# The last Fourier layer's second complex mixing by three real products, and scan records loaded three chunks ahead

## The chip, the cores and the metric

The kernel runs on one core of one Trainium2 chip. The metric is the device time of one execution in microseconds. A core has TensorE (PE, its weight loads are PEld), VectorE (DVE), ScalarE (ACT), GpSimd (POOL) and SyncE (SP), which issues most of the transfers.

## What is computed

Four layers over `x` of 4 x 512 x 64 x 64, each behind a group normalisation and with a residual path folded in: a recurrent layer with test-time training (a scan over 256 chunks of 16 tokens), a Fourier layer, a channel gate, and a second Fourier layer. The change touches the first and the last:

```python
# scan, one chunk of 16 tokens for each of 8 heads and 4 images
Z1 = xk @ W1c + b1c
grad = _ln_l2_bwd(Z1, xv - xk, g, bb)
W1n = W1c - (last_eta * xk).swapaxes(-1, -2) @ grad
b1n = b1c - (last_eta * grad).sum(-2, keepdims=True)
...
# Fourier layer
spec = jnp.fft.rfft2(x, axes=(2, 3), norm='ortho')
xr, xi = (out.real, out.imag)
or_ = einsum('bkihw,kio->bkohw', ar, w[0]) - einsum('bkihw,kio->bkohw', ai, w[1]) + b[0]
oi_ = einsum('bkihw,kio->bkohw', ai, w[0]) + einsum('bkihw,kio->bkohw', ar, w[1]) + b[1]
o1r, o1i = relu(cmul(xr, xi, w1, b1))
o2r, o2i = cmul(o1r, o1i, w2, b2)
out_c = (o2r + 1j * o2i) * origin
return jnp.fft.irfft2(out_c, s=(H, W), axes=(2, 3), norm='ortho')
```

## The kernel before

Everything is fp32. `fourier_back` is the last Fourier layer. It works on 16 units (4 images x 4 groups of 128 channels), one after the other; channels lie on the partitions. A unit's half spectrum is `spec[k]`, 33 slots of 64 frequencies, real and imaginary. It is mixed in NCH = 9 chunks: six of 256 columns, then three of 192. Each chunk goes through these steps:

- `mix1`: three real products on TensorE (`once1` = w_re times (x_re + x_im) in `psA[0]`, and two more in `psA[1]`), with the sum x_re + x_im made by GpSimd (`sums`);
- `copy_once1` on ScalarE takes `once1` out of PSUM, `combine_hidden` on VectorE adds it to both halves of `psA[1]`, and `relu` on ScalarE (two activations) makes `hidden[q]`;
- `mix2`: four real products on TensorE, two into `psB[0]` and two into `psB[1]`;
- `terms` on VectorE: four scalar_tensor_tensor, each adding the bias to a half of `psB` and multiplying by a half of `spec`, into `prod[q]`;
- `gate` on GpSimd: one difference and one sum of `prod[q]`, back into `spec[k]`.

While unit u is mixed, the rows of unit u - 1 (still in `half`) are transformed back, one batch of 512 columns a chunk: transposes (`turn_rows`), `evacuate` on ScalarE, products (`transform_rows`), `row_back` on VectorE. Behind the nine chunks the columns of unit u follow (`turn_columns`, `transform_columns`). The first unit has no rows to turn. Every engine runs a fixed list of instructions in program order, and semaphores (`Signal`, here counted by step) join them. TensorE's list in a chunk is mix2(c), transform_rows(c), turn_rows(c+2), mix1(c+2); mix2(c) waits for hidden(c) and for terms(c-1).

`scan_and_read` is the recurrent layer. Chunk s of the scan works on `record[s % 4]`, a 392 KB load from HBM (`load_record`, a ring of RING = 4). The recurrence is kept for two groups g of two images. TensorE transposes the keys of the next chunk (`turn_keys`, L2299), multiplies keys by the state (`project_k`) and adds to the state (`update`, L2328); the signal `state_ps[g]` counts the updates. SyncE goes chunk by chunk (`body`): the load of a later record (L1840), the tiles' loads and stores, and the two stores of the gradients, each of which waits for its `stored_sb[g]`. Records are `turn_keys`'d late in an odd chunk, and early in an even one.

Of the kernel before, what the change touches and what calls it, by code (L numbers as in the profile page):

```python
# [649 lines left out]
def fourier_back(nc, name, s_in, x_out, weights, biases, d, coef):  # L650

    o_view = x_out.rearrange("b (k c) h w -> (b k) c (h w)", c=P)
# [6 lines left out]
    with ExitStack() as ctx:  # L659
# [12 lines left out]
        wdif = sb("weights_dif", [P, CT, P])  # L672
# [6 lines left out]
        hidden = [sb(f"hidden{k}", [P, 2, CW]) for k in range(2)]  # L679
        once1 = sb("once1", [P, CW])  # L680
        prod = [sb(f"prod{k}", [P, 2, 2, CW]) for k in range(2)]
# [28 lines left out]
        mix2_ps = sig("mix2_ps", 2 * NCH)  # L710
# [67 lines left out]
        def _(pool):  # L778
            def combine_weights(ct):
                pool.wait_ge(w_loaded[ct].sem, w_loaded[ct].at(0, 32))  # L780
                nc.gpsimd.tensor_tensor(wneg[:, ct], zeros[:], wt[:, ct, 0:4:3], ALU.subtract).then_inc(neg_begun.sem, 1)  # L781
                nc.gpsimd.tensor_tensor(wdif[:, ct], wt[:, ct, 1], wt[:, ct, 0], ALU.subtract)
                pool.wait_ge(neg_begun.sem, neg_begun.at(0, ct + 1))
                nc.gpsimd.tensor_tensor(wneg[:, ct, 0], wneg[:, ct, 0], wt[:, ct, 1], ALU.subtract).then_inc(combined.sem, 1)

            def sums(u, k):
                pool.wait_ge(mix1_ps.sem, mix1_ps.at(u, 0))
                for n, (s0, s1) in enumerate(PARTS):
                    pool.wait_ge(scaled.sem, scaled.at(u, n + 1))
                    if n == 0:  # L790
                        pool.wait_ge(dc_added.sem, dc_added.at(u, 1))
                    nc.gpsimd.tensor_tensor(xsum[:, s0:s1], spec[k][:, s0:s1, 0, :], spec[k][:, s0:s1, 1, :],  # L792
                                            ALU.add).then_inc(xsum_sb.sem, 1)

# [12 lines left out]
            def unit(u, it, k, ct, first):  # L807
                cf = coef[:, bass.ds(u, 1), :].rearrange("p o e -> p (o e)")
                nc.gpsimd.tensor_tensor(bias_re[k][:], bias[:, ct, 2:3], cf[:, 2:3], ALU.add).then_inc(bias_made.sem, 1)
                sums(u, k)  # L810
                if first:
                    for n in range(1, CT):
                        combine_weights(n)
                for c in range(NCH):
                    gate(u, k, (k * NCH + c) % 2, c, cf)
# [6 lines left out]
        def _(act):  # L822
# [21 lines left out]

            def relu(u, k, ct, c):
                n = width(c)
                q = (k * NCH + c) % 2
                act.wait_ge(pre_sb.sem, pre_sb.at(u, c + 1))
                for r in range(2):
                    done = nc.scalar.activation(hidden[q][:, r, 0:n], hidden[q][:, r, 0:n], ACT.Relu, bias=bias[:, ct, r:r + 1])  # L850
                done.then_inc(hidden_sb.sem, 1)
# [4 lines left out]
            def unit(u, it, k, ct, first, final=False):  # L856
# [5 lines left out]
                for c in range(NCH):  # L862
                    if not first and c + 2 < NB1:
                        row_back(u, k, c + 2)
                    if c + 2 < NCH:
                        copy_once1(u, c + 2)
                        relu(u, k, ct, c + 2)
# [16 lines left out]
        def _(dve):  # L884
# [17 lines left out]
            def terms(u, k, q, c, adds):  # L902
                s0, s1 = CHUNKS[c]
                n = width(c)
                dve.wait_ge(prod_sb.sem, prod_sb.at(u, c - 1))
                for r, add in enumerate(adds):
                    dve.wait_ge(mix2_ps.sem, mix2_ps.at(u, 2 * c + r + 1))
                    src = psB[r][:, 0:n].rearrange("p (s h) -> p s h", h=H)
                    for e in range(2):
                        done = v.scalar_tensor_tensor(prod[q][:, r, e, 0:n].rearrange("p (s h) -> p s h", h=H), src, add,  # L910
                                                      spec[k][:, s0:s1, e, :], ALU.add, ALU.mult)
                done.then_inc(terms_sb.sem, 1)

            def unit(u, it, k, ct, first):
# [3 lines left out]
                for c in range(NCH):  # L918
                    q = (k * NCH + c) % 2
                    terms(u, k, q, c, (bias_re[k][:], bias[:, ct, 3:4]))  # L920
                    if c < NB1 and not first:
                        row_back(u, it, k, c)
                    if c + 2 < NCH:
# [15 lines left out]
        def _(pe):  # L939
# [34 lines left out]
            def mix1(u, k, ct, c):  # L974
# [7 lines left out]
                pe.matmul(psA[1][:, CW:CW + n], wdif[:, ct], x[:, :, 0, :], start=True, stop=True).then_inc(mix1_ps.sem, 1)  # L982

            def mix2(u, k, ct, c):
# [3 lines left out]
                if c:  # L988
                    pe.wait_ge(terms_sb.sem, terms_sb.at(u, c))
                for r, (wa, wb) in enumerate(((wt[:, ct, 2], wneg[:, ct, 1]), (wt[:, ct, 3], wt[:, ct, 2]))):  # L990
                    pe.matmul(psB[r][:, 0:n], wa, hidden[q][:, 0, 0:n], start=True, stop=False)  # L991
                    pe.matmul(psB[r][:, 0:n], wb, hidden[q][:, 1, 0:n], start=False, stop=True).then_inc(mix2_ps.sem, 1)  # L992
# [630 lines left out]
def scan_and_read(nc, T, d, x_in, rec, q_in, grad, x_out, chan_stats):  # L1623
# [15 lines left out]
    with ExitStack() as ctx:  # L1639
# [198 lines left out]
        def _(sp):  # L1838
# [26 lines left out]
            for s in range(2):  # L1865
# [4 lines left out]
            def body(at, scan):  # L1870
                s, c, v, p = at.s, at.c, at.v, at.p
                if scan:

                    for g in range(GR):
                        sp.wait_ge(state_ps[g].sem, state_ps[g].at(s, -1))
                    load_record((c + 2) % RING, s + 2)
# [25 lines left out]
            for r in range(RING):  # L1902
                sp.wait_ge(rec_in[r].sem, rec_in[r].at(SC * 2 + (r < 2), 0))
# [827 lines left out]
```

## Time and profile before

| | before |
|---|---|
| runs, us | 5644.74, 5626.67, 5643.87 (median 5643.87) |
| the profiled execution | 5642.43 us, its span 5640.3 us |
| PE / DVE / ACT / POOL busy | 93% / 74% / 46% / 48% of the span |
| mean granted TensorE clock | 0.971 |
| scan, 1579 to 3850 us | 2271 us |
| last Fourier layer's units, 4838.5 us to the end | 801.8 us |

The busy share says how much of the span an engine had an instruction in work. TensorE's records overlap and their ends are modelled, so for it the distance from start to start is the better measure of what an instruction costs; for the other engines it is the distance too where two follow each other without a wait.

### The profile page before, as it was taken

How to read it: one execution, taken by the hardware profiler on the slowest of the kernel's cores; microseconds unless marked ns; L12 is line 12 of the kernel's file. 1: busy time of each engine (PE TensorE's matmuls, PEld its weight loads, DVE VectorE, ACT ScalarE, POOL GpSimd, SP SyncE). 2: the span in 40 equal slices, each digit the busy share in tenths (PEclk: the TensorE clock that was granted, in tenths of full speed). 3: DMA queues.
4: the chain of work that ended last, by engine and by line, in shares of the span. 5: the costliest groups of instructions: out<-in, count | busy, mean ns of one | idle time of the engine just before them, and what ended most of it. 6: DMA issues, size and time to landing. Idle time of an engine off the chain costs nothing. (4 is left out here: it accounts for less than half of the span.)

```text
span 5640.3 us, 144710 instructions
## 1 busy us (share of the span) xinstructions
PE 5236.2 (93%) x44534; PEld 4008.5 (71%) x44534; DVE 4165.7 (74%) x14714; ACT 2613.6 (46%) x7573; POOL 2684.5 (48%) x4382
## 2 busy tenths in 40 slices
PE   5999999999969999999999999997999997799999
PEld 2444444444448888888888888886888896699888
DVE  4766667656558888888888888886788888566665
ACT  0111111111146666666666666664555554454444
POOL 1444444444435655565556565662444444333332
PEclk8999999999959999999999999998999999899999
DMA  4434444333324444444444444443312121222121
GB/s 182 163 123 156 149 148 163 125 118 125 117 80 119 123 123 123 121 123 122 121 122 122 120 122 118 123 124 88 131 77 92 78 92 47 88 92 80 76 90 76
DMA packets 599465, 645.80 MB, mean 114 GB/s; under 512 B 172976, under 2 KB 503096, under 8 KB 587736
## 3 DMA queue, kind: packets, MB, share of 16 engines
q1 hardware_dynamic: 440712, 491.44, 27.4%
q10 hardware_dynamic: 157904, 144.22, 7.6%
q8 instruction: 390, 6.39, 0.5%
q14 instruction: 459, 3.76, 0.2%
HBM read 357.56 MB, written 278.00 MB: 113 GB/s over the span
## 5 line engine op out<-in xcount | busy, mean ns | idle before, releaser
L1613 PE MATMUL proj_ps<-proj_w_sb,proj_h 128*128 128x512 f32 x3072 | 1347.2, 596 | 0.0
L1613 PEld LDWEIGHTS proj_ps<-proj_w_sb,proj_h 128*128 128x128 f32 x3072 | 577.4, 190 | 743.4 <-issue 724.7
L1516 DVE SCALAR_TENSOR_TENSOR proj_lin<-proj_ps,proj_rstd,proj_wbias_sb 128x512 f32<-128x512 f32 x384 | 283.0, 746 | 496.9 <-PE proj_ps L1613 490.9
L1928 POOL TENSOR_TENSOR scan_b_step<-scan_core,scan_rate_last 128x128 f32<-128x128 f32 x512 | 325.3, 635 | 631.4 <-DVE scan_core L2188 631.4
L2397 PE MATMUL scan_ps_y<-scan_o_t,proj_wo_sb 128*128 128x128 f32 x4096 | 569.7, 282 | 2.1 <-ACT scan_o_t L2031 2.1
L2397 PEld LDWEIGHTS scan_ps_y<-scan_o_t,proj_wo_sb 128*128 128x128 f32 x4096 | 500.0, 192 | 32.6 <-ACT scan_o_t L2031 2.6
L1997 ACT ACTIVATE scan_square<-scan_ps_z 128x64 f32<-128x64 f32 x1024 | 219.9, 220 | 490.5 <-PE scan_ps_z L2316 464.3
L1431 POOL TENSOR_TENSOR proj_gk<-proj_rec,proj_gain_sb 128x256 f32<-128x256 f32 x256 | 181.4, 730 | 529.5 <-DVE proj_rec L1537 529.5
L1425 POOL TENSOR_TENSOR proj_by_cos<-proj_lin,proj_rope 128x512 f32<-128x512 f32 x256 | 335.4, 1324 | 164.8 <-DVE proj_lin L1516 123.1
L2328 PE MATMUL scan_ps_w<-scan_step,scan_record 64*128 64x128 f32 x4088 | 359.1, 296 | 9.0 <-DVE scan_step L2193 8.7
L1936 POOL TENSOR_TENSOR scan_b_sum<-scan_b_step,scan_b_sum 128x128 f32<-128x128 f32 x512 | 318.4, 622 | 46.5 <-POOL scan_b_step L1928 8.6
L1990 ACT COPY scan_state_w<-scan_ps_w 128x512 f32<-128x512 f32 x480 | 279.1, 582 | 121.0 <-PE scan_ps_w L2328 118.7
L2328 PEld LDWEIGHTS scan_ps_w<-scan_step,scan_record 64*128 64x128 f32 x4088 | 278.7, 193 | 40.4 <-DVE scan_step L2193 14.2
L418 DVE SCALAR_TENSOR_TENSOR fourier_boxes<-fourier_spec,fourier_tab 128x256 f32<-128x256 f32 (+3 forms) x544 | 302.5, 593 | 0.5
L550 PE MATMUL fourier_psD<-fourier_mats,fourier_turned 128*128 128x128 f32 x2148 | 291.9, 278 | 11.0 <-DVE fourier_spec L452 8.4
L288 POOL TENSOR_TENSOR fourier_spec<-fourier_prod 128x256 f32<-128x256 f32 (+1 forms) x144 | 129.6, 900 | 356.5 <-DVE fourier_prod L439 356.5
L800 POOL TENSOR_TENSOR fourier_spec<-fourier_prod 128x256 f32<-128x256 f32 (+1 forms) x144 | 98.4, 683 | 411.6 <-DVE fourier_prod L910 411.6
L550 PEld LDWEIGHTS fourier_psD<-fourier_mats,fourier_turned 128*128 128x128 f32 x2148 | 273.4, 193 | 23.0 <-ACT fourier_turned L319 14.8
L2167 DVE TENSOR_TENSOR scan_zg<-scan_ps_z,scan_gain 128x128 f32<-128x128 f32 x512 | 146.0, 285 | 187.1 <-ACT scan_square L1997 162.4
L951 PE MATMUL fourier_psD<-fourier_mats,fourier_turned 128*128 128x128 f32 x2080 | 277.6, 277 | 4.1 <-ACT fourier_turned L826 4.1
L951 PEld LDWEIGHTS fourier_psD<-fourier_mats,fourier_turned 128*128 128x128 f32 x2080 | 262.0, 191 | 14.2 <-ACT fourier_turned L826 8.1
L826 ACT COPY fourier_turned<-fourier_psT 128x512 f32<-128x512 f32 (+1 forms) x272 | 153.6, 566 | 244.1 <-PE fourier_psT L943 244.1
(326 smaller groups left out, 13269.3 us busy)
## 6 DMA issues: line engine op xcount, KB each, us to landing
scan_record<-records SPq DMA_DIRECT2D x258, 392.0 KB
records<-proj_rec ACTq DMA_DIRECT2D x256, 392.0 KB, 3.7
spectra<-fourier_spec SPq DMA_DIRECT2D x16, 2112.0 KB, 6.5
fourier_spec<-spectra SPq DMA_DIRECT2D x16, 2112.0 KB, 8.7
proj_h<-x SPq DMA_DIRECT2D x32, 1024.0 KB, 6.5
queries<-proj_q ACTq DMA_DIRECT2D x128, 256.0 KB, 3.7
gradients<-scan_stored SPq DMA_DIRECT2D x512, 64.0 KB
scan_q_in<-queries SPq DMA_DIRECT2D x128, 256.0 KB, 7.7
```

The costliest lines, as they stand in the source:

```text
L418: v.scalar_tensor_tensor(boxes[:, g % 2, 0:nj * 2 * nf].rearrange("p (j e f) -> p j e f", j=nj, e=2), spec[q][:, s, :, f], 1.0, tab[:, j, ...
L550: done = pe.matmul(psD[t % 2][:, col:col + P], turned[t % 2][:, j * P:(j + 1) * P], mat, start=True, stop=True)
L951: done = pe.matmul(psD[q][:, col:col + P], turned[q][:, j * P:(j + 1) * P], mat, start=n == 0, stop=n == len(terms) - 1)
L1425: g_.tensor_tensor(by_cos[q][:, n].rearrange("p (a e) -> p a e", e=32), lin[q][:, n].rearrange("p (a e) -> p a e", e=32), cos, ALU.mult).t ...
L1516: v.scalar_tensor_tensor(lin[q][:, n], ps[q][n][:], rstd[k][:, j:j + 1], T.wbias[:, n], ALU.mult, ALU.add).then_inc(lin_sb.sem, 1)
L1613: last = pe.matmul(ps[j % 2][n][:], h[k][:, ct, j * P:(j + 1) * P], T.w[:, n, ct], start=ct == 0, stop=ct == CT - 1)
L1928: v.tensor_tensor(b_step[g][:], core[g][:], rate_last[g][:, :, 2:3].broadcast_to([P, PB, HD]), ALU.mult).then_inc(b_step_sb[g].sem, 1)
L1936: v.tensor_tensor(b_sum[g][(c + 1) % RING][:], b_step[g][:], b_sum[g][c % RING][:], ALU.add).then_inc(b_sum_sb[g].sem, 1)
L1990: a.copy(state_of(g, at)[:].rearrange("p r b a e -> p r (b a e)"), ps_w[:, :, g].rearrange("p r b a e -> p r (b a e)")).then_inc(state_sb[ ...
L1997: a.activation(square[:, g, b], ps_z[g][:, b * HD:(b + 1) * HD], ACT.Square, accum_out=ssq[g][:, b:b + 1]).then_inc(ssq_sb[g].sem, 1)
L2328: done = pe.matmul(ps_w[:, r, g, b].rearrange("p a e -> p (a e)"), record[at.ring][rows, PB * g + b, 0:2 * HD], step[g][rows, b].rearrange ...
L2397: pe.matmul(ps_y[:, n], T.wo[:, ct, n * P:(n + 1) * P], o_t[:, ct], start=ct == 0, stop=False)
```

## The change

In `fourier_back` the second mixing is done like the first: GpSimd makes `hsum` = h_re + h_im (`sum_hidden`), TensorE makes three products (`psB[1]` holds two, `psB[0]` the one with `hsum`), ScalarE takes the latter out of PSUM (`copy_once2`), and VectorE adds bias, `psB[1]` and `once2` into `mixed` in SBUF (`combine_mixed`) and multiplies it by the spectrum with two tensor_tensor of 512 columns (`terms`), both of whose inputs are in SBUF. `mix2(c)` waits for `mixed(c-1)` in place of terms(c-1), and its last product for `hsum`. In the scan, three records are loaded ahead in place of two, and the load waits for all updates up to the chunk before in place of the one before that.

```diff
+            def sum_hidden(u, q, c):
+                n = width(c)
+                pool.wait_ge(hidden_sb.sem, hidden_sb.at(u, c + 1))
+                if c >= 2:
+                    pool.wait_ge(mix2_ps.sem, mix2_ps.at(u, c - 1))
+                nc.gpsimd.tensor_tensor(hsum[q][:, 0:n], hidden[q][:, 0, 0:n], hidden[q][:, 1, 0:n], ALU.add).then_inc(hsum_sb.sem, 1)
...
                 for c in range(NCH):
-                    gate(u, k, (k * NCH + c) % 2, c, cf)
+                    sum_hidden(u, (k * NCH + c) % 2, c)
+                    if c:
+                        gate(u, k, (k * NCH + c - 1) % 2, c - 1, cf)
+                gate(u, k, (k * NCH + NCH - 1) % 2, NCH - 1, cf)
...
+            def copy_once2(u, c):
+                n = width(c)
+                act.wait_ge(mix2_ps.sem, mix2_ps.at(u, c + 1))
+                nc.scalar.copy(once2[:, 0:n], psB[0][:, 0:n]).then_inc(once2_sb.sem, 1)
...
                 for c in range(NCH):
+                    copy_once2(u, c)
                     if not first and c + 2 < NB1:
                         row_back(u, k, c + 2)
                     if c + 2 < NCH:
...
-            def terms(u, k, q, c, adds):
+            def combine_mixed(u, q, c, adds):
+                n = width(c)
+                dve.wait_ge(once2_sb.sem, once2_sb.at(u, c + 1))
+                for r, add in enumerate(adds):
+                    done = v.scalar_tensor_tensor(mixed[q][:, r, 0:n], psB[1][:, r * CW:r * CW + n], add, once2[:, 0:n],
+                                                  ALU.add, ALU.add)
+                done.then_inc(mixed_sb.sem, 1)
+
+            def terms(u, k, q, c):
                 s0, s1 = CHUNKS[c]
                 n = width(c)
+                dve.wait_ge(mixed_sb.sem, mixed_sb.at(u, c + 1))
                 dve.wait_ge(prod_sb.sem, prod_sb.at(u, c - 1))
-                for r, add in enumerate(adds):
-                    dve.wait_ge(mix2_ps.sem, mix2_ps.at(u, 2 * c + r + 1))
-                    src = psB[r][:, 0:n].rearrange("p (s h) -> p s h", h=H)
-                    for e in range(2):
-                        done = v.scalar_tensor_tensor(prod[q][:, r, e, 0:n].rearrange("p (s h) -> p s h", h=H), src, add,
-                                                      spec[k][:, s0:s1, e, :], ALU.add, ALU.mult)
+                for r in range(2):
+                    pv = prod[q][:, r, :, 0:n].rearrange("p e (s h) -> p e s h", h=H)
+                    mv = mixed[q][:, r, 0:n].rearrange("p (s h) -> p s h", h=H).unsqueeze(1).broadcast_to([P, 2, s1 - s0, H])
+                    done = v.tensor_tensor(pv, mv, spec[k][:, s0:s1].rearrange("p s e h -> p e s h"), ALU.mult)
                 done.then_inc(terms_sb.sem, 1)
...
                     q = (k * NCH + c) % 2
-                    terms(u, k, q, c, (bias_re[k][:], bias[:, ct, 3:4]))
+                    combine_mixed(u, q, c, (bias_re[k][:], bias[:, ct, 3:4]))
                     if c < NB1 and not first:
                         row_back(u, it, k, c)
+                    terms(u, k, q, c)
                     if c + 2 < NCH:
                         combine_hidden(u, q, c + 2)
...
                 if c:
-                    pe.wait_ge(terms_sb.sem, terms_sb.at(u, c))
-                for r, (wa, wb) in enumerate(((wt[:, ct, 2], wneg[:, ct, 1]), (wt[:, ct, 3], wt[:, ct, 2]))):
-                    pe.matmul(psB[r][:, 0:n], wa, hidden[q][:, 0, 0:n], start=True, stop=False)
-                    pe.matmul(psB[r][:, 0:n], wb, hidden[q][:, 1, 0:n], start=False, stop=True).then_inc(mix2_ps.sem, 1)
+                    pe.wait_ge(mixed_sb.sem, mixed_sb.at(u, c))
+                pe.matmul(psB[1][:, 0:n], wneg[:, ct, 1], hidden[q][:, 1, 0:n], start=True, stop=True)
+                pe.matmul(psB[1][:, CW:CW + n], wdif[:, ct, 1], hidden[q][:, 0, 0:n], start=True, stop=True)
+                pe.wait_ge(hsum_sb.sem, hsum_sb.at(u, c + 1))
+                pe.matmul(psB[0][:, 0:n], wt[:, ct, 2], hsum[q][:, 0:n], start=True, stop=True).then_inc(mix2_ps.sem, 1)
...
-            for s in range(2):
+            for s in range(3):
                 load_record(s, s)
...
                     for g in range(GR):
-                        sp.wait_ge(state_ps[g].sem, state_ps[g].at(s, -1))
-                    load_record((c + 2) % RING, s + 2)
+                        sp.wait_ge(state_ps[g].sem, state_ps[g].at(s, 0))
+                    load_record((c + 3) % RING, s + 3)
```

Left out: the buffers and signals that these lines name, the weights' sums for the second mixing (`wneg`, `wdif`, made by GpSimd), and the last waits of SyncE.

On ScalarE, inside a unit's chunks, a chunk's work before is one transposed batch out (`fourier_turned`), one `once1` (from `psA`) and the two activations of relu:

```order
L850 ACTIVATE fourier_hidden<-fourier_hidden,fourier_bias 128x256 x2
L826 COPY fourier_turned<-fourier_psT 128x512
L843 COPY fourier_once<-fourier_psA 128x256
L850 ACTIVATE fourier_hidden<-fourier_hidden,fourier_bias 128x256 x2
L826 COPY fourier_turned<-fourier_psT 128x512
```

The same place in the changed kernel; `fourier_once<-fourier_psB` is `once2`:

```order
L873 ACTIVATE fourier_hidden<-fourier_hidden,fourier_bias 128x256 x2
L866 COPY fourier_once<-fourier_psB 128x256
L844 COPY fourier_turned<-fourier_psT 128x512
L861 COPY fourier_once<-fourier_psA 128x256
L873 ACTIVATE fourier_hidden<-fourier_hidden,fourier_bias 128x256 x2
L866 COPY fourier_once<-fourier_psB 128x256
```

The copy of `once2` for chunk c + 1 stands right behind the relu of chunk c + 2.

On VectorE, the same chunk before (`fourier_prod` is terms, `fourier_x` is row_back, `fourier_hidden` is combine_hidden of chunk c + 2):

```order
L910 SCALAR_TENSOR_TENSOR fourier_prod<-fourier_psB,fourier_bias_re,fourier_spec 128x256 x2
L907 REGISTER_ALU
L910 SCALAR_TENSOR_TENSOR fourier_prod<-fourier_psB,fourier_bias,fourier_spec 128x256 x2
L891 REGISTER_ALU
L892 COPY fourier_x<-fourier_psD 128x512
L896 REGISTER_ALU
L899 TENSOR_TENSOR fourier_hidden<-fourier_psA,fourier_once 128x512
```

And after (`fourier_mixed` is combine_mixed):

```order
L930 SCALAR_TENSOR_TENSOR fourier_mixed<-fourier_psB,fourier_bias_re,fourier_once 128x256
L930 SCALAR_TENSOR_TENSOR fourier_mixed<-fourier_psB,fourier_bias,fourier_once 128x256
L915 REGISTER_ALU
L916 COPY fourier_x<-fourier_psD 128x512
L942 TENSOR_TENSOR fourier_prod<-fourier_mixed,fourier_spec 128x512 x2
L920 REGISTER_ALU
L923 TENSOR_TENSOR fourier_hidden<-fourier_psA,fourier_once 128x512
```

Two of the four scalar_tensor_tensor are gone, two tensor_tensor of twice the width stand behind row_back, and combine_hidden of chunk c + 2 is still the last of a chunk.

## Rows read from the trace of the kernel before

**Rows 1.** The page: busy time of each engine, share of the span, instructions.
```profile
PE 5236.2 (93%) x44534; PEld 4008.5 (71%) x44534; DVE 4165.7 (74%) x14714; ACT 2613.6 (46%) x7573; POOL 2684.5 (48%) x4382
```

**Rows 2.** Windows, busy us of PE PEld DVE ACT POOL, clock: scan, last Fourier.
```profile
1579.00:3850.00 2271.00, 2147.31 (x29634) 1863.80 (x29633) 1910.14 (x9628) 1519.47 (x5322) 1335.87 (x2803) 0.97 0.42 119
4838.50:5640.30 801.80, 766.23 (x5129) 714.53 (x5127) 502.70 (x991) 379.58 (x791) 280.00 (x402) 0.99 0.21 81
```

**Rows 3.** Waits of PE in the scan: total us, times, longest us.
```profile
PE scan_ps_turn L2299 <- DMA scan_record<-records: 64.8, 72, 3.6
...
PE scan_ps_z L2316 <- ACT scan_k_t L2005: 9.1, 33, 0.7
PE scan_ps_w L2328 <- DVE scan_step L2193: 8.7, 15, 1.7
```

**Rows 4.** Timeline of PE in the scan, four chunks: start us, length us.
```profile
2335.59 0.65 PE L2299 MATMUL scan_ps_turn<-proj_ident_sb,scan_record 128*128 128x128 f32 x4
...
2337.87 0.71 PE L2328 MATMUL scan_ps_w<-scan_step,scan_record 64*128 64x128 f32 x8
...
2348.21 0.72 PE L2328 MATMUL scan_ps_w<-scan_step,scan_record 64*128 64x128 f32 x8
...
2352.34 0.66 PE L2299 MATMUL scan_ps_turn<-proj_ident_sb,scan_record 128*128 128x128 f32 x4
...
2357.52 0.66 PE L2299 MATMUL scan_ps_turn<-proj_ident_sb,scan_record 128*128 128x128 f32 x4 [0.87 <-DMA scan_record<-records]
...
2370.18 0.66 PE L2299 MATMUL scan_ps_turn<-proj_ident_sb,scan_record 128*128 128x128 f32 x4
```

**Rows 5.** Timeline of SyncE's queue in the same chunks.
```profile
2339.85 0.62 SPq L1840 DMA_DIRECT2D scan_record<-records  x1
...
2349.70 0.62 SPq L1840 DMA_DIRECT2D scan_record<-records  x1
```

**Rows 6.** Timeline of PE in one unit's mixing, last Fourier layer.
```profile
5171.15 0.60 PE L991 MATMUL fourier_psB<-fourier_hidden,fourier_weights 128*128 128x256 f32 x2
...
5184.21 0.59 PE L991 MATMUL fourier_psB<-fourier_hidden,fourier_weights 128*128 128x256 f32 x2
5184.64 0.59 PE L992 MATMUL fourier_psB<-fourier_hidden,fourier_weights_neg 128*128 128x256 f32 x2
...
5188.56 0.59 PE L991 MATMUL fourier_psB<-fourier_hidden,fourier_weights 128*128 128x256 f32 x2
...
5203.56 1.04 PE L943 MATMUL fourier_psT<-fourier_ident,fourier_spec 128*128 128x128 f32 x8
```

**Rows 7.** Timelines of DVE and ACT there; the last two rows: another unit.
```profile
5184.48 0.69 DVE L899 TENSOR_TENSOR fourier_hidden<-fourier_psA,fourier_once 128x512 f32<-128x512 f32 x1 [1.11 <-PE fourier_psA L982]
5185.20 0.91 ACT L850 ACTIVATE fourier_hidden<-fourier_hidden,fourier_bias 128x256 f32<-128x256 f32 x2 [1.23 <-DVE fourier_hidden L899]
5185.27 0.88 DVE L910 SCALAR_TENSOR_TENSOR fourier_prod<-fourier_psB,fourier_bias_re,fourier_spec 128x256 f32<-128x256 f32 x2
...
5187.03 0.69 DVE L892 COPY fourier_x<-fourier_psD 128x512 f32<-128x512 f32 x1
...
4879.36 0.91 ACT L850 ACTIVATE fourier_hidden<-fourier_hidden,fourier_bias 128x256 f32<-128x256 f32 x2
4880.17 0.36 ACT L843 COPY fourier_once<-fourier_psA 128x256 f32<-128x256 f32 x1
```

**Rows 8.** Groups by form: busy us, mean ns, idle before.
```profile
L418 DVE SCALAR_TENSOR_TENSOR fourier_boxes<-fourier_spec,fourier_tab 128x256 f32<-128x256 f32 x306 | 238.5, 814 | 0.0
...
L1506 DVE TENSOR_TENSOR proj_rec<-proj_gk,proj_lin 128x512 f32<-128x512 f32 x128 | 103.1, 806 | 10.3 <-POOL proj_rec L1432 9.0
...
L2246 DVE TENSOR_TENSOR scan_zn<-scan_zgain,scan_hrstd 128x512 f32<-128x512 f32 x128 | 88.6, 692 | 4.4
...
L899 DVE TENSOR_TENSOR fourier_hidden<-fourier_psA,fourier_once 128x384 f32<-128x384 f32 x48 | 26.8, 558 | 29.7 <-PE fourier_psA L982 29.7
...
L801 POOL TENSOR_TENSOR fourier_spec<-fourier_prod 128x256 f32<-128x256 f32 x96 | 69.8, 727 | 0.0
```

More of the change, by code:

```diff
@@ L671, in fourier_back @@
         wneg = sb("weights_neg", [P, CT, 2, P])
-        wdif = sb("weights_dif", [P, CT, P])
+        wdif = sb("weights_dif", [P, CT, 2, P])
         bias = sb("bias", [P, CT, 4])
@@ L679, in fourier_back @@
         hidden = [sb(f"hidden{k}", [P, 2, CW]) for k in range(2)]
+        hsum = [sb(f"hsum{k}", [P, CW]) for k in range(2)]
         once1 = sb("once1", [P, CW])
+        once2 = sb("once2", [P, CW])
+        mixed = [sb(f"mixed{k}", [P, 2, CW]) for k in range(2)]
         prod = [sb(f"prod{k}", [P, 2, 2, CW]) for k in range(2)]
@@ L709, in fourier_back @@
         hidden_sb = sig("hidden_sb", NCH)
-        mix2_ps = sig("mix2_ps", 2 * NCH)
+        hsum_sb = sig("hsum_sb", NCH)
+        mix2_ps = sig("mix2_ps", NCH)
+        once2_sb = sig("once2_sb", NCH)
+        mixed_sb = sig("mixed_sb", NCH)
         terms_sb = sig("terms_sb", NCH)
@@ L780, in combine_weights @@
                 pool.wait_ge(w_loaded[ct].sem, w_loaded[ct].at(0, 32))
-                nc.gpsimd.tensor_tensor(wneg[:, ct], zeros[:], wt[:, ct, 0:4:3], ALU.subtract).then_inc(neg_begun.sem, 1)
-                nc.gpsimd.tensor_tensor(wdif[:, ct], wt[:, ct, 1], wt[:, ct, 0], ALU.subtract)
+                re, im = wt[:, ct, 0:4:2], wt[:, ct, 1:4:2]
+                nc.gpsimd.tensor_tensor(wneg[:, ct], zeros[:], re, ALU.subtract).then_inc(neg_begun.sem, 1)
+                nc.gpsimd.tensor_tensor(wdif[:, ct], im, re, ALU.subtract)
                 pool.wait_ge(neg_begun.sem, neg_begun.at(0, ct + 1))
-                nc.gpsimd.tensor_tensor(wneg[:, ct, 0], wneg[:, ct, 0], wt[:, ct, 1], ALU.subtract).then_inc(combined.sem, 1)
+                nc.gpsimd.tensor_tensor(wneg[:, ct], wneg[:, ct], im, ALU.subtract).then_inc(combined.sem, 1)
             def sums(u, k):
@@ L981, in mix1 @@
                 pe.matmul(psA[1][:, 0:n], wneg[:, ct, 0], x[:, :, 1, :], start=True, stop=True)
-                pe.matmul(psA[1][:, CW:CW + n], wdif[:, ct], x[:, :, 0, :], start=True, stop=True).then_inc(mix1_ps.sem, 1)
+                pe.matmul(psA[1][:, CW:CW + n], wdif[:, ct, 0], x[:, :, 0, :], start=True, stop=True).then_inc(mix1_ps.sem, 1)
             def mix2(u, k, ct, c):
@@ L1902, in _ @@
             for r in range(RING):
-                sp.wait_ge(rec_in[r].sem, rec_in[r].at(SC * 2 + (r < 2), 0))
+                sp.wait_ge(rec_in[r].sem, rec_in[r].at(SC * 2 + (r < 3), 0))
             for g in range(GR):
```

## The prediction

> **What bounds the kernel now.** I read the page first: TensorE is busy for 93% of the span, the others for half to three quarters [rows 1]. The change touches two stages, so I took a window of each [rows 2]. In both TensorE is the engine without gaps: 2147 of 2271 us in the scan, 766 of 802 us in the last Fourier layer, at a granted clock of 0.97 and 0.99. There the reader is to see that only what TensorE does, or waits for, sets the time.
>
> What it waits for in the scan is in the list of waits [rows 3]: 64.8 us, in 72 waits, for the record that the transposes of L2299 read. All else that is named there is under 10 us each. The timeline shows one such wait and one chunk pair without it [rows 4]: from 2335.59 to 2352.34, two chunks take 16.75 us; from 2352.34 to 2370.18, with a wait that is named with 0.87 us, 17.84 us. The record came late because its load was issued at 2349.70 [rows 5] and the transposes began at 2357.52, that is 7.8 us later, as soon as it had landed.
>
> In the last Fourier layer a chunk takes 4.35 us of TensorE (5184.21 to 5188.56), and of these a product of 256 columns takes 0.43 us (5184.21 to 5184.64) [rows 6]. In the same chunk VectorE works 0.69 + 2 x 0.88 + 0.69 = 3.1 us and waits for TensorE for the rest; ScalarE's relus take 0.91 us [rows 7]. From the first product of mix2(0) to the first transpose behind mix2(8) it is 32.41 us (5171.15 to 5203.56) [rows 6].
>
> **The scan.** The load of record s + 3 now waits for the updates of chunk s - 1, and stands where that of s + 2 stood. Either way it refills the ring's buffer that the update of four chunks before set free; what moves is its place in SyncE's queue, one chunk earlier. Is SyncE held up there, with the stores and loads behind it? The update of the second group ended at 2337.87 + 0.71 = 2338.58 and at 2348.21 + 0.72 = 2348.93 [rows 4], and SyncE came to its loads at 2339.85 and 2349.70 [rows 5]: the new wait is over before SyncE arrives, so it costs nothing, and would cost what little those two are apart if the stores were faster. The load that TensorE waited for at 2357.52 would be issued at 2339.85 in place of 2349.70, 9.9 us earlier; the wait of 0.87 us is covered ten times over. So the row's 64.8 us go at the most, or up to 80 if each of the 72 costs 0.2 us more than it is named with, as the pair above does (17.84 - 16.75 = 1.09). At the least nothing is gained, if another wait follows at once. Against that stands the pair without the wait: it ran in 16.75 us with the same work. I take **-62 us**.
>
> **The Fourier layer, TensorE alone.** Of four products one goes: per unit 6 x 0.43 and 3 x 0.33 (in proportion to 192 columns), 3.6 us, 57 us over 16 units. That would be the gain if TensorE stayed the bound.
>
> **The Fourier layer, the new chain.** ScalarE copies `once2` of chunk c + 1 behind the relu of chunk c + 2 (the order shown above). That relu waits for combine_hidden(c + 2), which VectorE does last in chunk c, behind combine_mixed(c), row_back(c) and terms(c). And combine_mixed(c + 1) waits for the copy. So from one combine_mixed to the next everything is in series, with nothing of it overlapped:
>
> - combine_mixed: two scalar_tensor_tensor with one input in PSUM and one in SBUF, as now two of L910: 0.88 us [rows 7];
> - row_back 0.69 us and combine_hidden 0.69 us, as now [rows 7];
> - terms: two tensor_tensor of 128x512 with both inputs in SBUF. The nearest row, the same form with a broadcast input, is 692 ns; the same form under much work of GpSimd is 806 ns [rows 8]. I take 0.69, so 1.38 us; the other end is 1.61;
> - relu: 0.03 us from combine_hidden's end (5184.48 + 0.69 to 5185.20), then 0.91 us [rows 7];
> - the copy of once2: as that of once1, 0.36 us, begun 0.10 us before the relus' record ends (4879.36 + 0.91 against 4880.17) [rows 7];
> - hand-off from ScalarE to VectorE: 0.06 us, my estimate, from 0.03 in the row above and up to 0.1.
>
> The sum is 4.9 us a chunk of 256 columns. TensorE has 4.35 - 0.43 = 3.92 us of work in it and waits for mixed(c) for 1.0 us. GpSimd has three operations of 0.73 us [rows 8], 2.2 us: hsum right behind the relus and over before TensorE's third product needs it, the gate behind terms. Nobody waits for GpSimd.
>
> A unit, from mix2(0) on: three products 1.29, 0.16 until the last is in PSUM, the copy 0.36 and the hand-off 0.06 make 1.9 us to combine_mixed(0). Then four steps of 4.9; the fifth with combine_hidden at 558 ns [rows 8] in place of 692 and relus narrower in proportion, 4.66; the sixth 4.6; the seventh with combine_mixed and terms of 192 columns, 4.2. Behind them combine_mixed(7) 0.74, a hand-off of 0.06 and three products of 0.33 make 1.8. The sum is 1.9 + 19.6 + 4.66 + 4.6 + 4.2 + 1.8 = 36.7 us against 32.4: **+4.3 us a unit**, 65 us over 15 units. The first unit has no row_back: a chunk goes from seven products, 3.0 us, to 4.2 us, about +6 us. The columns behind the mixing are as before, and they cover terms(8) and gate(8), which end later now by some 2 us. Together **+71 us**. The bounds: with terms at 1.61 us, +30 more (0.23 x 9 x 15); with overlaps of records that I have not credited (0.1 at each pair of like instructions, 0.2 a chunk), 27 less.
>
> The few sums of weights on GpSimd lie ahead of the first unit or behind its `sums`: under 2 us, within the rest.
>
> **Sum.** On the profiled execution's 5642.4 us (1.5 under the median of the runs): 5642.4 + 71 - 62 = **5651 us**. Two large terms nearly cancel. What a measurement of this kernel can tell from no change is 0.3%, 17 us: from 5627 to 5661 it is the same.
>
> **The rivals.**
>
> *Terms collide with GpSimd.* The new tensor_tensor read two inputs in SBUF, where L910 read one. A row of this kernel with two inputs in SBUF beside a busy GpSimd, L418, takes 814 ns for 256 columns, where L910 takes 0.44 [rows 7, 8]: 0.37 more. Paid by both operations in 144 chunks it is +107 us: 5758 us. It decides if GpSimd has an operation in work when terms starts. By the chain above it has not: hsum is over 0.4 us after combine_mixed starts, and the gate waits for terms. Chance 0.07. The page "SBUF — State Buffer" of the Trainium skill, section "Who interferes with whom", gives such a rule: a VectorE instruction with two SBUF inputs and a GpSimd instruction that reads SBUF exclude each other. L418 agrees, but no row of before has this meeting in the last layer.
>
> *The scan does not give back what it waits.* Another wait takes the record's place: ScalarE's key copy or VectorE's step, 9 us each now [rows 3], grow as TensorE comes earlier; VectorE is busy for 1910 of 2271 us [rows 2], 84%, and would be at 87%. Then the scan gains 15 us and the result is 5642 + 71 - 15 = 5698 us. Against it: the pair at 16.75 us. Chance 0.17.
>
> *A shorter chain and all of the waits.* Overlaps uncredited above (-27) and -78 in the scan: 5608 us. Chance 0.22.
>
> *The chain does not bind*, TensorE stays the bound and the change is what it says: 5642 - 57 - 62 = 5523 us. It needs ScalarE's copy ahead of the relu, which the order denies. Chance 0.06.
>
> The forecast itself has 0.48, with a range of its own from 5630 to 5672.
>
> **How the numbers follow.** The range reaches over the forecast, the scan's rival and the shorter chain: 5600 to 5705, and leaves out the collision and the chain that doesn't bind. Faster by over 0.3%: most of 0.22 and 0.06, 0.25. Slower: 0.17 + 0.07 and the upper third of the near cases, 0.32. Same: 0.43.
>
> **What the profile after would show.** In the last layer: TensorE's busy share down from 96% to about 83%, its waits there named with fourier_mixed, some 1.0 us each; ScalarE's copy of once2 right behind the relus; the distance between two combine_mixed 4.9 us; terms at 0.69 us; the mixing of a unit 36.7 us. In the scan: no wait of L2299 for the record, 16.75 us a pair, 2209 us in all. I am wrong if the once2 copy is not behind the relu, if terms is over 0.75 us, if TensorE falls to the lower clock in its 1.0 us waits, or if another wait stands where the record's stood.

## The result: 0.9% faster, and the profile after

The changed kernel takes 5586.5 us (median of 4 runs, 5580.0 to 5592.0), the one before 5641.4 us in the same comparison (4 runs, 5626.7 to 5644.7). The ratio is 0.9907, with a 95% interval from 0.9886 to 0.9928: 55 us faster. The forecast was 5651 us with a range from 5600 to 5705, so the time lies under the range.

The page of the changed kernel (its span is 5584.1 us), which answers to [rows 1]:

```profile
PE 5170.9 (93%) x44246; PEld 3939.1 (71%) x44246; DVE 4205.8 (75%) x14714; ACT 2642.5 (47%) x7717; POOL 2782.7 (50%) x4526
```

The windows of the two stages after, which answer to [rows 2] (stretch, its length, busy us of PE, PEld, DVE, ACT and POOL, granted clock, DMA share, GB/s):

```profile
1579.00:3755.00 2176.00, 2109.06 (x29640) 1845.25 (x29638) 1911.77 (x9633) 1520.26 (x5324) 1337.28 (x2806) 0.99 0.44 125
4741.80:5584.10 842.30, 738.21 (x4848) 662.77 (x4848) 533.38 (x992) 410.08 (x939) 382.94 (x551) 0.98 0.20 79
```

The scan's window went from 2271 to 2176 us with VectorE's busy time unchanged (1910 and 1912 us). The last Fourier layer grew from 802 to 842 us, and TensorE now has 738 us of records in it, 28 fewer than before, and many more gaps. Measured more closely, by the starts of the key transposes of the first and the last chunk, the scan went from 2265.5 to 2169.7 us, **-96**; by the first product of the first unit and the end, the last layer went from 806.6 to 842.3 us, **+36**. All that lies outside these two stages, which the change does not touch, is together 4 us longer, with no row that explains it. On the profiled execution's 5642.4 us that makes 5586, and the profiled execution after took 5586.3 us. Both stage figures are of one execution before and one after. That matters for the scan: the five other kernels below that have the new loads took 2171.4 to 2178.0 us for the same scan, and the one with the old loads 2253.0 in place of 2265.5, so by the traces the scan gained between 75 and 96 us.

TensorE's waits in the scan after (line, what it waited for: total us, times, longest), which answer to [rows 3]:

```profile
PE scan_ps_w L2361 <- DVE scan_step L2226: 17.9, 25, 1.7
PE scan_ps_z L2342 <- issue: 17.3, 6, 3.3
```

The wait for the record, 64.8 us in 72 times before, is not in the list any more. The wait for VectorE's step, the rival's candidate, grew from 8.7 to 17.9 us: possibly some of what the record's wait hid. The transposes of the keys in the timeline of PE, which answer to [rows 4], and the records' loads in SyncE's queue, which answer to [rows 5], both some 430 us further on in the scan:

```profile
2763.77 0.60 PE L2332 MATMUL scan_ps_turn<-proj_ident_sb,scan_record 128*128 128x128 f32 x4
...
2780.51 0.60 PE L2332 MATMUL scan_ps_turn<-proj_ident_sb,scan_record 128*128 128x128 f32 x4
```

```profile
2764.07 0.97 SPq L1873 DMA_DIRECT2D scan_record<-records  x1
...
2768.20 4.34 SPq L1918 DMA_DIRECT2D gradients<-scan_stored  x2
```

From 2763.77 to 2780.51 a pair of chunks takes 16.74 us. The record that is used at 2780.51 was issued at 2764.07, 16.4 us ahead. For the same chunk of the kernel before, load and use were 2828.13 and 2835.60, 7.5 us apart, with a named wait:

```profile
2828.13 0.62 SPq L1840 DMA_DIRECT2D scan_record<-records  x1
```

```profile
2835.60 0.66 PE L2299 MATMUL scan_ps_turn<-proj_ident_sb,scan_record 128*128 128x128 f32 x4 [1.01 <-DMA scan_record<-records]
```

Over the scan the median distance from load to use for these chunks (every other one) went from 8.1 to 17.1 us, and for those between from 13.2 to 19.4 us. SyncE's own waits show what the load was moved past:

```profile
SPq L1918 <- POOL scan_stored L1972: 958.0, 417, 4.7
```

In the last layer the list of TensorE's waits (after the first products) is led by the new chain:

```profile
PE fourier_psB L1022 <- DVE fourier_mixed L930: 63.3, 82, 2.1
```

That is 0.8 us for one wait, where 1.0 was forecast. TensorE is busy for 88% of this stage (738 of 842 us), where about 83% was forecast.

And here is a turn of it, in the timelines of DVE and ACT, which answer to [rows 7]:

```profile
5110.08 0.48 DVE L930 SCALAR_TENSOR_TENSOR fourier_mixed<-fourier_psB,fourier_bias_re,fourier_once 128x256 f32<-128x256 f32 x1 [1.23 <-ACT fourier_once L866]
5110.48 0.47 DVE L930 SCALAR_TENSOR_TENSOR fourier_mixed<-fourier_psB,fourier_bias,fourier_once 128x256 f32<-128x256 f32 x1
5110.87 0.68 DVE L916 COPY fourier_x<-fourier_psD 128x512 f32<-128x512 f32 x1
5111.47 1.28 DVE L942 TENSOR_TENSOR fourier_prod<-fourier_mixed,fourier_spec 128x512 f32<-128x512 f32 x2
5112.67 0.68 DVE L923 TENSOR_TENSOR fourier_hidden<-fourier_psA,fourier_once 128x512 f32<-128x512 f32 x1
5113.39 0.91 ACT L873 ACTIVATE fourier_hidden<-fourier_hidden,fourier_bias 128x256 f32<-128x256 f32 x2 [2.58 <-DVE fourier_hidden L923]
5114.20 0.35 ACT L866 COPY fourier_once<-fourier_psB 128x256 f32<-128x256 f32 x1
5114.58 0.48 DVE L930 SCALAR_TENSOR_TENSOR fourier_mixed<-fourier_psB,fourier_bias_re,fourier_once 128x256 f32<-128x256 f32 x1 [1.23 <-ACT fourier_once L866]
```

Every link stands in the order that the prediction gave, and each names the one before it: VectorE idles 1.23 us for ScalarE's copy, and ScalarE idles 2.58 us for combine_hidden. From 5110.08 to 5114.58 a chunk takes 4.50 us, not 4.9. The records' lengths are the ones forecast (terms 1.28 for two, relus 0.91, copy 0.35). But an instruction of VectorE that has nothing to wait for starts about 0.08 us before the record ahead of it ends: 5112.67 lies before 5111.47 + 1.28 = 5112.75, and 5111.47 before 5110.87 + 0.68 = 5111.55.

TensorE in the same unit, where the products of one chunk begin:

```profile
5111.10 0.67 PE L1022 MATMUL fourier_psB<-fourier_hidden,fourier_weights_neg 128*128 128x256 f32 x2
...
5115.61 0.67 PE L1022 MATMUL fourier_psB<-fourier_hidden,fourier_weights_neg 128*128 128x256 f32 x2 [0.35 <-DVE fourier_mixed L930]
```

The last waits 0.35 us by name, and the distance is 4.51 us. mix2(0) to the first transpose behind mix2(8) takes 34.2 us, where it took 32.4 (median of the 16 units, each from its first product) and 36.7 was forecast. This is what "a unit's mixing" means below; the expectations give it 0.1 to 0.2 us longer.

### The profile page after: what moved, and what is told of

The parts are those of the page before. It is cut to its first block and busy times, and to the rows that moved or that the text cites. A ratio compares the mean times of both kernels' runs of the same rounds, so it can differ in the third digit from the quotient of the medians.

```text
span 5584.1 us, 144447 instructions
## 1 busy us (share of the span) xinstructions
PE 5170.9 (93%) x44246; PEld 3939.1 (71%) x44246; DVE 4205.8 (75%) x14714; ACT 2642.5 (47%) x7717; POOL 2782.7 (50%) x4526
## 5 line engine op out<-in xcount | busy, mean ns | idle before, releaser
L2361 PE MATMUL scan_ps_w<-scan_step,scan_record 64*128 64x128 f32 x4088 | 354.4, 293 | 18.2 <-DVE scan_step L2226 17.9
L288 POOL TENSOR_TENSOR fourier_spec<-fourier_prod 128x256 f32<-128x256 f32 (+1 forms) x144 | 128.5, 892 | 358.6 <-DVE fourier_prod L439 358.6
L2226 DVE TENSOR_TENSOR scan_step<-scan_core,scan_rate_last 128x256 f32<-128x256 f32 x512 | 218.2, 426 | 62.1 <-DVE scan_core L2221 0.9
L1559 DVE TENSOR_TENSOR proj_by_sin<-proj_lin,proj_rope 128x256 f32<-128x256 f32 x512 | 261.8, 573 | 0.0
L2208 DVE SCALAR_TENSOR_TENSOR scan_t_row<-scan_zg,scan_rstd,scan_record 128x64 f32<-128x64 f32 x1024 | 261.0, 295 | 0.0
```

Of the source, the lines that this page charges most:

```text
L1559: last = v.tensor_tensor(o2[:, :, t], x2[:, :, 1 - t], sin, ALU.mult)
L2361: done = pe.matmul(ps_w[:, r, g, b].rearrange("p a e -> p (a e)"), record[at.ring][rows, PB * g + b, 0:2 * HD], step[g][rows, b].rearrange ...
```

## The experiments

Each time is a median, followed by the ratio to the kernel before and its 95% interval. The first four are compared with the kernel before at 5638.4 us (7 runs), the last three with the same kernel at 5636.6 us (12 runs). The distances in the traces are taken as above.

**One half of the change at a time.** The first kernel has the old mixing and the new loads; against the kernel before, its edit is:

```diff
-            for s in range(2):
+            for s in range(3):
                 load_record(s, s)
...
-                        sp.wait_ge(state_ps[g].sem, state_ps[g].at(s, -1))
-                    load_record((c + 2) % RING, s + 2)
+                        sp.wait_ge(state_ps[g].sem, state_ps[g].at(s, 0))
+                    load_record((c + 3) % RING, s + 3)
```

> The kernel before with the records' part alone. By the traces the scan is 96 us shorter after the change (2265.5 us from the first to the last key transpose before, 2169.7 after) and nothing else of that part moves: 5641 - 96 = 5545 us. Rival: the two parts help each other and the scan alone gives only the 62 us that I forecast: 5580 us.

Measured: 5553.8 us, 0.9854 (0.9838 to 0.9870), 85 us faster, 9 us short of the 5545 that the traces had promised. The scan took 2178.0 us, the last layer 806.9 as before. The second kernel keeps the new mixing and has the old loads; against the changed kernel:

```diff
-            for s in range(3):
+            for s in range(2):
                 load_record(s, s)
...
-                        sp.wait_ge(state_ps[g].sem, state_ps[g].at(s, 0))
-                    load_record((c + 3) % RING, s + 3)
+                        sp.wait_ge(state_ps[g].sem, state_ps[g].at(s, -1))
+                    load_record((c + 2) % RING, s + 2)
```

> The changed kernel with the records' part taken back, so the mixing alone. By the traces the last Fourier layer is 36 us longer: 5641 + 36 = 5677 us. Forecast of the prediction: 5641 + 71 = 5712 us. Rival (the layer gains and something else lost it): under 5641 us.

Measured: 5672.8 us, 1.0069 (1.0052 to 1.0086), 34 us slower. The last layer took 844.3 us, the scan 2253.0. The two halves add up to -50 us, the whole change to -55. Each of these is uncertain by some 10 us, so no effect of one half on the other is to be seen. So both terms of the forecast had the right sign and the wrong size: by these times the scan was off by 23 us (-85 for -62) and the layer by 37 (+34 for +71), both to the same side.

**Does ScalarE's order make the chain?** One line is moved, so that once2 of the next chunk is copied ahead of the relus for which ScalarE waits:

```diff
+                copy_once2(u, 0)
                 for c in range(NCH):
-                    copy_once2(u, c)
...
+                    if c + 1 < NCH:
+                        copy_once2(u, c + 1)
+                    if c + 2 < NCH:
                         relu(u, k, ct, c + 2)
```

> The changed kernel with one move on ScalarE: the copy of once2 of chunk c + 1 stands ahead of the relu of chunk c + 2 in place of behind it. Same instructions, same work on every engine. If the chain combine_mixed, row_back, terms, combine_hidden, relu, copy sets the period of 4.5 us, it is cut, TensorE is the bound again at 3.92 us a chunk, a unit's mixing goes from 34.3 to some 29 us, and the time from 5586 to about 5505 us. Rival, VectorE is the bound by its work or the collision with GpSimd: the move gains under 20 us.

Measured: 5506.3 us, 0.9772 (0.9756 to 0.9788), as expected. The last layer took 765.9 us, 41 less than before the change, a unit's mixing 29.2 us. The timelines of DVE and ACT of this kernel:

```profile
5056.03 0.48 DVE L933 SCALAR_TENSOR_TENSOR fourier_mixed<-fourier_psB,fourier_bias_re,fourier_once 128x256 f32<-128x256 f32 x1 [1.38 <-ACT fourier_once L866]
...
5059.95 0.48 DVE L933 SCALAR_TENSOR_TENSOR fourier_mixed<-fourier_psB,fourier_bias_re,fourier_once 128x256 f32<-128x256 f32 x1 [0.64 <-ACT fourier_once L866]
```

```profile
5059.55 0.37 ACT L866 COPY fourier_once<-fourier_psB 128x256 f32<-128x256 f32 x1 [1.73 <-PE fourier_psB L1028]
5059.82 0.91 ACT L873 ACTIVATE fourier_hidden<-fourier_hidden,fourier_bias 128x256 f32<-128x256 f32 x2
```

Now the copy waits for TensorE, no longer for VectorE, and a chunk takes 3.92 us, which is TensorE alone, as the prediction had it for a chain that does not bind. TensorE's wait for `mixed` shrank from 63.3 us to the last row here:

```profile
PE fourier_psA L1015 <- DVE fourier_hidden L926: 10.0, 19, 0.9
...
PE fourier_psB L1028 <- POOL fourier_hsum L808: 2.9, 1, 2.9
PE fourier_psB L1025 <- DVE fourier_mixed L933: 1.4, 2, 1.3
```

The place of one copy is worth 76 us of the last layer (842.3 to 765.9): the chain was what the new mixing cost, and it hung on that place.

**The same chain cut elsewhere.** VectorE gets combine_hidden(c + 2) ahead of terms(c), which takes terms out of the chain:

```diff
                         row_back(u, it, k, c)
-                    terms(u, k, q, c)
                     if c + 2 < NCH:
                         combine_hidden(u, q, c + 2)
+                    terms(u, k, q, c)
```

> The changed kernel with one move on VectorE: combine_hidden of chunk c + 2 stands ahead of terms of chunk c, ScalarE's order as changed. If the chain is the cause, taking the 1.2 us of terms out of it makes it shorter than TensorE's 3.92 us: 5505 to 5515 us, nearly as in the move on ScalarE. If it is ScalarE's order alone that costs (relu ahead of once2 for another reason), this one gains nothing: 5586 us.

Measured: 5520.2 us, 0.9798 (0.9781 to 0.9814), 5 us over the expected stretch; the last layer took 782.2 us, a unit's mixing 30.2 us. TensorE's waits in its last layer:

```profile
PE fourier_psB L1025 <- POOL fourier_hsum L808: 11.0, 19, 2.7
PE fourier_psB L1022 <- DVE fourier_mixed L930: 9.0, 22, 1.3
```

This cuts the chain too, but now TensorE's third product waits for GpSimd's hsum, in 19 waits where it was one with the kernel above. Cutting either link is enough to end the 4.5 us; where the cut is made decides which wait is next.

**How far ahead must the load stand?** Three records ahead as in the change, but in SyncE's list behind the two gradient stores of the chunk instead of ahead of them:

```diff
-                    for g in range(GR):
-                        sp.wait_ge(state_ps[g].sem, state_ps[g].at(s, 0))
-                    load_record((c + 3) % RING, s + 3)
+                    pass
...
                                      stored[g][c % 2][:]).then_inc(grad_gone[g][c % 2].sem, 16)
+                    for g in range(GR):
+                        sp.wait_ge(state_ps[g].sem, state_ps[g].at(s, 0))
+                    load_record((c + 3) % RING, s + 3)
```

> The changed kernel, the load of record s + 3 moved behind the two gradient stores of chunk s in SyncE's queue: that is one place ahead of where before had it, ahead of the two loads of gradients (1.3 us) only. If TensorE waited for the last microsecond of a transfer of some 8 us, then 1.3 us earlier is nearly enough: the scan stays within 10 us of the change's 2170 us and the time at 5586 to 5596 us. Rival: the whole chunk of lead is needed (the transfer stretches with what runs beside it, or the third record preloaded matters): the scan goes back to some 2250 us and the time to some 5670 us.

Measured: 5632.3 us, 0.9994 (0.9984 to 1.0004). Neither the expectation nor its rival came true; the time lies between them. The scan took 2215.2 us, about half of its gain gone. One row of TensorE's waits in its scan, and one wait with its load in SyncE's queue:

```profile
PE scan_ps_turn L2333 <- DMA scan_record<-records: 30.1, 41, 2.0
```

```profile
2790.61 4.32 SPq L1916 DMA_DIRECT2D gradients<-scan_stored  x2
2795.26 0.61 SPq L1873 DMA_DIRECT2D scan_record<-records  x1
```

```profile
2804.19 0.66 PE L2333 MATMUL scan_ps_turn<-proj_ident_sb,scan_record 128*128 128x128 f32 x4 [1.10 <-DMA scan_record<-records]
```

The load stands 8.9 us ahead of its use and is late; the median distance is 8.8 and 12.0 us, about as in the kernel before (8.1 and 13.2), although the program says three chunks ahead. The stores ahead of it wait for GpSimd, and they are worth a chunk of lead: against the changed kernel the medians are 8.3 and 7.4 us less. So about half of the gain hangs on the load's place ahead of them. The other half stayed, although the load that is waited for, that of every other chunk, is by the median issued only 0.7 us earlier than in the kernel before; why so little is worth so much is not shown. It also gives a second price of the record's wait: 45.5 us of scan for 30.1 us named, where the kernel before paid 95.9 us for 64.8.

**GpSimd in the first unit.** The changed kernel's GpSimd makes nine sums of weights between `sums` and the first hsum. Its timeline (the nine end at 4751.86), and the product that waits:

```profile
4745.72 0.72 POOL L789 TENSOR_TENSOR fourier_weights_neg<-fourier_zeros,fourier_weights 128x256 f32<-128x256 f32 x1
...
4751.86 1.41 POOL L808 TENSOR_TENSOR fourier_hsum<-fourier_hidden 128x256 f32<-128x256 f32 x2
```

```profile
4752.64 0.70 PE L1025 MATMUL fourier_psB<-fourier_hsum,fourier_weights 128*128 128x256 f32 x2 [2.54 <-POOL fourier_hsum L808]
```

On top of the earlier copy of once2, I spread the nine, three each, behind chunks 1, 3 and 5:

```diff
-                if first:
-                    for n in range(1, CT):
-                        combine_weights(n)
...
+                    if first and c in (1, 3, 5):
+                        combine_weights(c // 2 + 1)
```

> The changed kernel with once2's copy ahead of the relu (as in the move on ScalarE before), and the sums of weights of the other three channel groups on GpSimd moved from ahead of the first unit's first hsum to behind its second, fourth and sixth. In the changed kernel these nine operations of 0.72 us hold the first hsum until 4752 us and TensorE with it. Without it the first unit's mixing goes from 31.2 to some 26 us: 5501 us against 5506 with the move on ScalarE alone. Rival: the first unit pays for something else: no change.

Measured: 5513.9 us, 0.9789 (0.9772 to 0.9807), not faster than 5506.3. GpSimd's operations and TensorE in its first unit:

```profile
4752.98 0.72 POOL L789 TENSOR_TENSOR fourier_weights_neg<-fourier_zeros,fourier_weights 128x256 f32<-128x256 f32 x1
4753.66 1.17 POOL L790 TENSOR_TENSOR fourier_weights_dif<-fourier_weights 128x256 f32<-128x256 f32 x1
4754.80 1.17 POOL L792 TENSOR_TENSOR fourier_weights_neg<-fourier_weights_neg,fourier_weights 128x256 f32<-128x256 f32 x1
4755.93 0.71 POOL L808 TENSOR_TENSOR fourier_hsum<-fourier_hidden 128x256 f32<-128x256 f32 x1
```

```profile
4756.70 0.70 PE L1027 MATMUL fourier_psB<-fourier_hsum,fourier_weights 128*128 128x256 f32 x2 [2.35 <-POOL fourier_hsum L808]
```

And VectorE's terms at the same time:

```profile
4752.98 2.41 DVE L944 TENSOR_TENSOR fourier_prod<-fourier_mixed,fourier_spec 128x512 f32<-128x512 f32 x2
```

One wait of 2.9 us became three, 6.5 us in all, because three sums now stand ahead of an hsum in each of three chunks. And they meet terms: the two tensor_tensor take 2.41 us where they take 1.28 alone, and the second and third sum, which run beside them, 1.17 us where they take 0.72. This is the collision of the prediction's rival, here where GpSimd has work when terms starts. It is there with the earlier copy alone too, in its first unit, where hsum stands beside terms:

```profile
4750.37 1.82 DVE L945 TENSOR_TENSOR fourier_prod<-fourier_mixed,fourier_spec 128x512 f32<-128x512 f32 x2
```

```profile
4750.57 1.07 POOL L808 TENSOR_TENSOR fourier_hsum<-fourier_hidden 128x256 f32<-128x256 f32 x1
```

The first unit's mixing took 34.6 us against 31.0. The rest of the difference is in stages that the edit does not touch, a few us each.

**Both cuts with it.** On top of the kernel with the weights spread:

```diff
-                    terms(u, k, q, c)
                     if c + 2 < NCH:
                         combine_hidden(u, q, c + 2)
+                    terms(u, k, q, c)
```

> As the kernel with the weights later, and combine_hidden also ahead of terms on VectorE. Both cuts of the chain at once: TensorE has no wait for mixed or hsum left, a unit's mixing is 29.0 to 29.4 us and the time is the same as with the one move, 5495 to 5503 us. Rival: terms behind combine_hidden ends too late for the gate or for the next combine_mixed, as where it was moved alone: 5510 us or more.

Measured: 5526.7 us, 0.9805 (0.9787 to 0.9822), the rival's case; a unit's mixing is 30.2 us, as with the second cut alone, and hsum is waited for 15.2 us in 18 times. With the copy early, terms is not in the way; moving it behind combine_hidden makes terms, and by it the gate and the next hsum in GpSimd's list, late. The best of all the kernels measured is the earlier copy alone, 5506.3 us.

## Why the prediction was wrong

The mechanisms were right, and two terms of the sum were mis-sized, both on the side of the slower time: **the Fourier layer +71 measured +36, the scan -62 measured -96** in the profiled executions, and about -85 in the times of the kernel with the new loads alone. By the profiled executions each was off by about 35 us, and not against each other: together 69 us, where the range reached 51 us down. With 85 for the scan it is still some 60.

- *The Fourier chain, right in every link, wrong in its sum.* The step that failed is the item list that adds combine_mixed 0.88, row_back 0.69, terms 1.38 and combine_hidden 0.69 end to end, 3.64 us; from the start of the first to the end of the last it is 5113.35 - 5110.08 = 3.27. At each of four seams about 0.08 us of two records overlap. From there on the steps held: relu 0.04 us later, copy 0.81 after it, 0.35 long, hand-off 0.03. The bound for overlaps was 0.2 us a chunk; measured were 0.4 with the hand-off. The rows of before misled me: in [rows 7] each of VectorE's groups starts at or behind the end of the one ahead, since each waits there for TensorE, and only inside the pair of L910 is the overlap to be seen: the two take 0.88 us, and one of them 479 ns.

```profile
L910 DVE SCALAR_TENSOR_TENSOR fourier_prod<-fourier_psB,fourier_bias_re,fourier_spec 128x256 f32<-128x256 f32 x192 | 84.1, 479 | 21.1 <-PE fourier_psB L992 16.2
```

  "Perfetto Trace Analysis" of the Trainium skill, section "Optimizing Scalar/DVE Operations", says that the write-acknowledgement half of a profiled VectorE instruction's access overhead overlaps with the next instruction, by its figures an estimate of some 60 ns for data in SBUF and some 125 ns for PSUM; the trace agrees in kind and has 80 ns, for row_back's copy out of PSUM too, less than that estimate for PSUM.
- *The unit's sum*, step by step: 1.90 us to the first combine_mixed (forecast 1.9), four turns of 4.505 (4.9), then 4.27 (4.66), 4.21 (4.6), 3.82 (4.2), and 1.9 behind the last turn (1.8): 34.2 us in place of 36.7. A unit was 1.75 us longer than before in place of 4.3; fifteen times that is 26 us in place of 65.
- *The first unit* was forecast with +6 us and took +9.7 (its mixing 25.0 us before, 34.7 after): 26 and 9.7 are the 36 us measured. It took 5.45 us to its first combine_mixed, where the forecast for a unit is 1.9. "Nobody waits for GpSimd" and "under 2 us" for the weights failed there: TensorE waited 2.5 us for hsum, and the granted clock was 0.54 in the 2 us ahead of that wait and 0.50 from 4754.0 to 4756.5 behind it, the lower of its two levels.
- *Terms at 0.69 us* was right: 684 ns in the mean over 192. The rival of a collision with GpSimd did not come in the changed kernel. Its condition, GpSimd in work when terms starts, was brought about by the spread sums of weights, and there its price was 1.13 us for two operations (2.41 against 1.28), more than the 0.37 each that the rival was given; beside an hsum, with the earlier copy, it was 0.54 us for two (1.82). The page "SBUF — State Buffer" of the Trainium skill, section "Who interferes with whom", says that a VectorE instruction with two SBUF inputs contends with a GpSimd instruction that reads SBUF; these rows agree.
- *The scan.* Of the intervals between two key transposes behind the first sixteen chunks, 66 held a wait for the record in the kernel before. They shrank by 63.5 us for 52.8 us of named waits: each cost about 0.16 us more than its name. With the 18.0 us of the first sixteen chunks this is about the 80 us of the prediction's upper bound. The step that failed is "so the row's 64.8 us go at the most, or up to 80": the pair in [rows 4] showed 1.09 against 0.87, and I took the smaller. TensorE's weight loads (PEld) wait for the same record, and their row had the larger figure:

```profile
PEld scan_ps_turn L2299 <- DMA scan_record<-records: 80.1, 78, 3.8
```

  The two kernels with one half of the change each agree: with the old loads this figure is 78.0 us (and that of the matmuls 59.0), and the scan with the new loads is 75.0 us shorter. What went beyond 80 us in the profiled executions before and after lies in the intervals between, 15.4 us, where no record is waited for. 8.2 us of it are one interval, of 21.2 us where its like takes 13.1, in which the granted clock fell. The window of that interval in the kernel before, with the granted clock third from the end:

```profile
3425.00:3447.00 22.00, 19.47 (x189) 16.94 (x189) 12.13 (x68) 11.22 (x42) 7.99 (x18) 0.69 0.39 102
```

  The kernel with the new mixing and the old loads has the same scan, and this interval takes it 13.6 us. So these 8 us are of one execution of the kernel before and not what its loads cost each time.
- *The scan's first chunks.* From 1579 to 1714 us the granted clock is 0.65 in the kernel before and 0.84 in the changed one:

```profile
1579.00:1714.00 135.00, 107.50 (x1289) 77.93 (x1289) 91.52 (x494) 66.83 (x249) 65.33 (x160) 0.65 0.28 84
```

```profile
1579.00:1714.00 135.00, 109.79 (x1546) 83.06 (x1544) 109.08 (x583) 81.00 (x296) 76.10 (x184) 0.84 0.32 96
```

  There 12 us of the record's waits went and the sixteen chunks became 18 us shorter, 132.0 to 114.0. These two are the ends of what the executions show. The other execution with the old loads has 0.74 and 129.6 us, the five others with the new ones 0.75 to 0.83 and 114.2 to 120.3 us, and the load behind the stores, with 7.7 us of waits, 0.72 and 124.4 us. So the chunks are shorter without the waits in every execution, but the clock's 0.74 with 12.6 us of waits and 0.75 with none lie side by side: that fewer waits raise the clock is not shown.
- *A row that was passed over.* "All else that is named there is under 10 us each" is not so: the list of TensorE's waits in the scan also has 16.6 us of "issue", in 6 times. It is 17.3 us after the change, so nothing in the sum hangs on it.
- *The rivals.* The time came nearest to "a shorter chain and all of the waits", 5608 us with a chance of 0.22, and went beyond it by longer overlaps and by the scan. "The scan does not give back what it waits" had the right candidate, the wait for VectorE's step, but it grew by 9 us and no more. "The chain does not bind" is true of the kernel with the earlier copy, which measured 5506 where that rival has 5523 us; its scan gained more than 62 us and its layer 41 us in place of 57.

## What to carry to other kernels

When an operation is split over more engines, write down each engine's list and follow the loop from one chunk to the next: a copy that stands behind an instruction that waits for another engine joins two chains into one, and moving that one line was worth 76 us here, more than the product saved. For such a loop take the distances from start to start where an engine has no wait, not the lengths of the records, and not rows in which it waits for another. A load's distance in chunks says little; what counts is which waiting instruction stands ahead of it in its queue, and a wait's time on TensorE's matmuls is its least price: here 64.8 us named were 75 to 96 us of the stage, and the waits of its weight loads for the same record, 80.1 us, were the better guess.

## What the runs showed of the hardware that was not expected

- fp32 VectorE instructions of 128x512, with no wait between them, follow each other in 0.60 us where the record is 0.68 us long: terms, with both inputs in SBUF, and row_back's copy, with its input in PSUM.
- VectorE's tensor_tensor with both inputs in SBUF, beside GpSimd's tensor_tensor on SBUF, both lengthen: two of VectorE's took 2.41 us in place of 1.28, and GpSimd's 1.17 in place of 0.72.
- A load of 392 KB was late when issued 7.5 or 8.9 us ahead of its use; in the changed kernel, where each is issued at least 16.1 us ahead behind the first sixteen chunks, and at least 11.9 us ahead in those, none is waited for.
- A wait for a record costs more than TensorE's matmuls name: 63.5 us of scan for 52.8 us named, 0.16 us for each of 66. The waits of the weight loads, 80.1 us in all, are nearer to what the scan gained.
- One interval of the scan took 21.2 us in one execution, at a granted clock of 0.69 over 22 us, and 13.6 us in another execution of the same scan.
